# Attention layer, 64 units of a head pair: pair weights loaded one unit sooner, and outputs scaled by VectorE straight from PSUM

## The reference, cut to what matters

```python
h = einsum('od,bdl->bol', Wq[i], z[:, :, s:e]) + einsum('od,bdl->bol', Wi[i], u[:, :, s:e])   # i: columns 0-255, 256-511
q, k, v = split(h)                        # 16 heads x 64 x 512 columns each
prob = softmax(einsum('bndi,bndj->bnij', q + r_w_bias, k) / 8)
attn = einsum('bnij,bndj->bndi', prob, v)
x = Wo @ attn + bo + z                    # then a normalisation over the 256 rows
```

## Time and profile before

| | |
|---|---|
| median of three runs | 3446.04 us |
| the profiled execution's own time | 3442.56 us |
| its span, first to last instruction | 3440.5 us |
| mean granted TensorE clock | 0.949 |
| TensorE busy | 3115.6 us (91%) |
| VectorE busy | 2362.2 us (69%) |
| ScalarE busy | 1742.2 us (51%) |
| GpSimd busy | 701.2 us (20%) |
| first layer | up to about 1312 us |

### The profile page before, as it was taken

How to read it: one execution, slowest core, us unless ns; L and a number is a source line. 1 busy time by engine, 2 the same in 40 slices (tenths; PEclk the granted TensorE clock), 3 DMA queues, 4 the chain that set the end, 5 groups by cost and what they waited for, 6 DMA issues and landing times. The chain is left out here.

```text
span 3440.5 us, 55581 instructions
## 1 busy us (share of the span) xinstructions
PE 3115.6 (91%) x20384; PEld 2400.2 (70%) x20384; DVE 2362.2 (69%) x3589; ACT 1742.2 (51%) x4185; POOL 701.2 (20%) x1207
## 2 busy tenths in 40 slices
PE   7998999999998996799999997589999999699998
PEld 6777777777777774566666664378887787488885
DVE  6776666666675662999999999257777888543212
ACT  4454444544454543355566553247777777432222
POOL 2444444544444441000000000011101111000000
PEclk9999999999999998899999998789999999899999
DMA  7668766666675655445555444210011110310004
GB/s 245 209 218 268 225 184 183 207 212 197 197 234 162 207 143 187 121 96 123 116 117 120 104 109 104 59 64 14 26 56 56 44 44 29 108 50 12 25 13 167
DMA packets 179676, 434.78 MB, mean 126 GB/s; under 512 B 52912, under 2 KB 61104, under 8 KB 154960
## 3 DMA queue, kind: packets, MB, share of 16 engines
q1 hardware_dynamic: 120256, 262.17, 26.9%
q10 hardware_dynamic: 28304, 106.09, 8.6%
q0 software_dynamic: 30848, 62.97, 7.3%
HBM read 233.95 MB, written 62.91 MB: 86 GB/s over the span
## 5 line engine op out<-in xcount | busy, mean ns | idle before, releaser
L281 POOL DMA_DIRECT2D l_probT<-l_prob x896 | 441.2, 500 | 258.6 <-DVE l_prob L778 238.8
L756 DVE TENSOR_REDUCE l_nmax<-l_bank 128x1 f32<-128x512 f32 x512 | 317.0, 681 | 198.2 <-PE l_bank L453 198.2
L576 ACT ACTIVATE l_prob<-l_bank,l_nmax 128x512 f32<-128x512 f32 x512 | 344.5, 688 | 135.1 <-DVE l_nmax L756 120.5
L419 PE MATMUL l_bank<-l_x_hi,l_w_hi 128*128 128x256 f32 x1024 | 307.6, 300 | 75.4 <-DMA l_w_lo<-kept_w_lo 54.5
L778 DVE STREAM_TRANSPOSE l_prob<-l_prob 128x1024 f32<-128x1024 f32 x256 | 314.4, 1228 | 16.3 <-DVE l_acc L799 9.7
L419 PE MATMUL l_bank<-l_x_hi,l_w_lo 128*128 128x256 f32 x1024 | 299.8, 293 | 0.0
L419 PE MATMUL l_bank<-l_x_lo,l_w_hi 128*128 128x256 f32 x1024 | 299.0, 292 | 0.0
L1817 DVE TENSOR_TENSOR_SCAN l_kv<-l_wx,l_kv 128x2056 f32<-128x2056 f32 x64 | 283.8, 4435 | 3.1 <-DVE l_sxc L1938 1.5
L419 PEld LDWEIGHTS l_bank<-l_x_hi,l_w_hi 128*128 128x128 f32 x1024 | 207.0, 202 | 99.5 <-DMA l_w_lo<-kept_w_lo 59.2
L2391 ACT ACTIVATE l2a_sc<-l2a_sc,l2a_nmax 128x256 f32<-128x256 f32 x512 | 254.7, 508 | 41.1 <-DVE l2a_nmax L2507 41.1
L478 PE MATMUL l_bank<-l_probT,l_v 128*64 128x256 f32 x2048 | 248.6, 397 | 25.9 <-issue 12.5
(11 more groups left out here) (348 smaller groups left out, 7989.3 us busy)
## 6 DMA issues: line engine op xcount, KB each, us to landing
l_probT<-l_prob SPq DMA_DIRECT2D x1152, 64.0 KB, 2.7
l_vb<-vd SPq DMA_DIRECT2D x64, 1024.0 KB
l_probT<-l_prob POOLq DMA_DIRECT2D x896, 64.0 KB, 2.4
l_w_hi<-kept_w_hi ACTq DMA_DIRECT2D x24, 1024.0 KB, 7.2
l_w_lo<-kept_w_lo ACTq DMA_DIRECT2D x24, 1024.0 KB, 7.7
l_wv_hi<-kept_wv_hi ACTq DMA_DIRECT2D x12, 1024.0 KB, 5.4
l_wv_lo<-kept_wv_lo ACTq DMA_DIRECT2D x12, 1024.0 KB, 5.6
kept_w_hi<-l_w_hi SPq DMA_DIRECT2D x8, 1024.0 KB, 9.8
```

The source lines that it names most:

```text
L281: eng.dma_start(probT[i % RING][r * SQ:(r + 1) * SQ, g, :, :, :, :], prob[i % RING][g * SQ:(g + 1) * SQ, r * IT:(r + 1) * IT, :, :, :]).th ...
L419: mm = pe.matmul(s.ap[:, c * ROWS:(c + 1) * ROWS], a[:, kt, c, g, :], b[:, kt, c * ROWS:(c + 1) * ROWS], start=m == 0, stop=m == 3 * KT - 1)
L576: act.activation(prob[i % RING][:, :, it % 2, h, :].rearrange("p (q t) s -> p t q s", q=Q), s.ap[:, :].rearrange("p (t q s) -> p t q s", t ...
L756: dve.tensor_reduce(nmax[:, n % 2, it, h:h + 1], s.ap[:, :], AX.X, ALU.max, negate=True).then_inc(max_ready, 1)
```

## The change

Three edits, all in the first layer.

1. `load_w` takes t = n // 2 + 2 and part l instead of t = (n - 1) // 2 + 2 and part 1 - l. The high part of t is issued in step 2t - 4 and the low part in 2t - 3. It waits for the key product of unit 2t - 3 only. The value weights have a function of their own, `load_wv`, in the steps in which they were issued before (2t - 3 and 2t - 2), now behind the w load of that step.
2. `weighed` and `outputs` of ScalarE and `scale_outputs` of GpSimd are gone. VectorE's `outputs(n)` multiplies o{n} in PSUM by rT twice, once into oT_hi (rounded) and once into oT, and subtracts. The bank o{n} is thus released by VectorE's second product.
3. VectorE's `outputs(n - 2)` moves in step n from behind `queries(n + 1)` to behind `maxima(n, (0, 1))`, ahead of the first two transposes. ScalarE's `sums(n)` waits for the release of o{n - 1} where it waited for GpSimd's product.

```diff
@@ GpSimd
-                def scale_outputs(n):
-                    drained(pool, S[f"o{n}"])
-                    drained(pool, S[f"r{n}"])
-                    pool.tensor_tensor(oT[:, :], oT[:, :], rT[:, :], ALU.mult).then_inc(scaled, 1)
-
                 for n in range(HALF + 2):
-                    if n > 1:
-                        scale_outputs(n - 2)
@@ ScalarE
                 def sums(n):
                     s = S[f"r{n}"]
                     full(act, s)
-                    act.wait_ge(scaled, n)
+                    if n:
+                        drained(act, S[f"o{n - 1}"])
                     act.activation(rT[:, :], s.ap[:, :], ACT.Copy).then_inc(s.drained, 1)
-
-                def weighed(n):
...
-                    act.activation(oT[:, :], s.ap[:, :], ACT.Copy).then_inc(s.drained, 1)
-
-                def outputs(n):
...
-                    act.activation(oT_hi[:, :], oT[:, :], ACT.Copy).then_inc(oT_hi_ready, 1)
@@
                 def load_w(t, part):
                     p, i = t % HP, t % 2
-                    projected(act, LANES * (t - 2) + 1)
-                    if i == 0:
-                        act.wait_ge(wv_stored, 32 * QUADS)
-                        act.dma_start((wv_hi, wv_lo)[part][:, :, :, :, :].bitcast(F32), wv_scratch[part][p // 2]).then_inc(wv_in, 16)
+                    full(act, S[f"k{LANES * (t - 2) + 1}"])
                     act.wait_ge(w_stored[i], 32 * QUADS)
                     act.dma_start((w_hi, w_lo)[part][i][:, :, :, :, :].bitcast(F32), w_scratch[part][p]).then_inc(w_in[i], 16)
+
+                def load_wv(g, part):
+                    projected(act, LANES * 2 * (g - 1) + 1)
+                    act.wait_ge(wv_stored, 32 * QUADS)
+                    act.dma_start((wv_hi, wv_lo)[part][:, :, :, :, :].bitcast(F32), wv_scratch[part][g % QUADS]).then_inc(wv_in, 16)
@@
-                    t = (n - 1) // LANES + 2
+                    t = n // LANES + 2
                     if HP <= t < TURNS * HP:
-                        load_w(t, 1 - l)
+                        load_w(t, l)
+                    t -= 1 - l
+                    if HP <= t < TURNS * HP and t % 2 == 0:
+                        load_wv(t // 2, 1 - l)
@@ VectorE
                 def outputs(n):
+                    s = S[f"o{n}"]
+                    full(dve, s)
+                    drained(dve, S[f"r{n}"])
+                    if n:
+                        full(dve, S[f"w{n - 1}_{RT - 1}"])
+                    dve.tensor_tensor(oT_hi[:, :], s.ap[:, :], rT[:, :], ALU.mult).then_inc(oT_hi_ready, 1)
+                    dve.tensor_tensor(oT[:, :], s.ap[:, :], rT[:, :], ALU.mult).then_inc(s.drained, 1)
+                    drained(dve, s)
                     dve.wait_ge(oT_hi_ready, n + 1)
                     dve.tensor_tensor(oT_lo[:, :], oT[:, :], oT_hi[:, :].bitcast(F32), ALU.subtract).then_inc(oT_ready, 1)
@@
                     maxima(n, (0, 1))
+                    if n > 1:
+                        outputs(n - 2)
                     turns(n, 0)
                     turns(n, 1)
                     if n + 1 < HALF:
                         queries(n + 1)
-                    if n > 1:
-                        outputs(n - 2)
```

More of the change, by code:

```diff
@@ L238, in l0_attention @@
         max_ready, rinv_ready, rows_ready = ph.sem("max_ready"), ph.sem("rinv_ready"), ph.sem("rows_ready")
-        scaled, oT_ready = ph.sem("scaled"), ph.sem("oT_ready")
+        oT_ready = ph.sem("oT_ready")
         acc_in = [ph.sem(f"acc_in{l}") for l in range(LANES)]
@@ L603, in sums @@
                     full(act, s)
-                    act.wait_ge(scaled, n)
+                    if n:
+                        drained(act, S[f"o{n - 1}"])
                     act.activation(rT[:, :], s.ap[:, :], ACT.Copy).then_inc(s.drained, 1)
-                def weighed(n):
[L608 to L611, removed]
-                    act.activation(oT[:, :], s.ap[:, :], ACT.Copy).then_inc(s.drained, 1)
-                def outputs(n):
-                    act.wait_ge(scaled, n + 1)
-                    if n:
-                        full(act, S[f"w{n - 1}_{RT - 1}"])
-                    act.activation(oT_hi[:, :], oT[:, :], ACT.Copy).then_inc(oT_hi_ready, 1)
                 def split_x(bp, l):
@@ L734, in _ @@
                         centred()
-                    if n:
-                        weighed(n - 1)
                     if n + 1 < HALF:
@@ L742, in _ @@
                         normed()
-                outputs(HALF - 2)
                 sums(HALF - 1)
-                weighed(HALF - 1)
-                outputs(HALF - 1)
                 act.wait_ge(xn_ready, RT)
```

## The result

| | before | after |
|---|---|---|
| median, us (4 runs each) | 3446.64 (3442.6 to 3448.65) | 3394.32 (3388.02 to 3410.31) |
| the profiled execution's own time | 3442.56 | 3398.0 |
| its span | 3440.5 | 3395.9 |
| mean granted TensorE clock | 0.949 | 0.953 |
| TensorE, VectorE busy | 3115.6, 2362.2 us | 3117.0, 2431.1 us |

The before column holds one run more than the three of the median 3446.04 (its time is 3447.24). The changed kernel is faster by 52 us: the ratio of the times is 0.9857, with a 95% interval of [0.982, 0.9893]. The forecast was 3406, so the gain is 12 us larger than predicted.

What follows compares the result with a forecast made beforehand. TensorE, busy 91%, was taken as the bound, losing time mostly to waits for the low weight part. Terms: -75 + 9.6 + 5 + 8.5 + 8 + 3.5 = -40.4 us, giving 3406 us, range 3384 to 3429.

Steps and rivals of the forecast that it cites:

- Loads one unit sooner: Ten long steps and step 51: TensorE's waits for the low weight part disappear, -75 us.
- ScalarE's copies and GpSimd's product go: First layer: TensorE's waits don't come from them, so removing them gains 0 us.
- The new wait of the key product: Steps 4g and 4g + 1 from step 16: k's bank waits for VectorE's second product, 0.4 us in 24 steps, +9.6.
- The input split: Steps 31 and alike: VectorE's late split of the next x is exposed by 1.6 us, three times, +5 (3 to 8).
- The moves behind the change of turn: Steps 19 and 35: 18 moves queue behind SyncE's wait for the stored accumulator, 4.2 us waited again, +8.5 (5 to 13).
- Turn 0: VectorE's added work delays weight splits, and a w load joins the stores of step 12: +8 us (2 to 14).
- Small ones: Steps 50 to 54 wait for ends 0.6 us later, +2; moves landing late in some long steps, +1.5; together +3.5.
- VectorE sets the pace: Rival, short steps: VectorE's load above 14.7 us per unit bounds the kernel, 3462 us; chance 5%.
- the early load collides: Rival, ten long steps: moves of the probabilities land later, weighing waits some 2.5 us each, 3431 us; chance 12%.
- the givebacks are hidden: Rival: the added costs stay at their lower bounds, 12 us, so the gain is 63, 3383 us; chance 16%.
- the load doesn't arrive sooner: Rival: a semaphore on ScalarE's queue holds the weight load, 3461 us; chance 2%.

Runs made afterwards that it cites:

- the loads alone: The kernel before with only the earlier weight loads (edit 1), ScalarE's copies and GpSimd's product kept: 3392.06 us, ratio 0.9855.
- the products alone: The changed kernel with the old `load_w`, so VectorE's products and the new place of `outputs` without the earlier loads: 3459.12 us, ratio 1.0047.
- the second trace: Trace of the changed kernel run again, unaltered, as the measure for later versions: 3400.14 us, ratio 0.9866.
- the last experiment: Changed kernel with next x's load moved, its split sooner, w's first high-part reload in step 13, outputs ahead of maxima from turn 1: 3380.72 us, ratio 0.9806.
- 1.15 us more: The changed kernel with two further VectorE subtractions per unit into tiles that nobody reads: 3420.76 us, ratio 0.9929.
- the outputs first: The changed kernel with VectorE's `outputs(n - 2)` ahead of the first maxima in all turns: 3399.67 us, ratio 0.9867.

## Why the prediction was right, point by point

The time fell as forecast, for the reason forecast: the waits for the weights went, and part of what they had covered came back. By terms, from the traces:

- *Loads one unit sooner, -75.* Steps 23, 39, 43, 59 at 20.67 us and the loads alone at 3392 us show it. No low part arrives late. Of what the Trainium skill says of the clock (TensorE: Matmul & The Clock Gate, "Loop structure matters more than you think"), the direction is borne out: without the waits the clock stays at 1.00 in these four steps.
- *ScalarE's copies and GpSimd's product go, 0.* In turns 1 to 3 right. In turn 0 wrong: steps 4 and 8 wait for moves, and they are shorter with the products in both pairs of kernels (28.5 and 28.0 before against 24.7 and 25.4 with the products alone). The way is not the one that the prediction named, that GpSimd's moves start sooner. In the traces GpSimd's moves for the first half have landed 1.0 us (before) and 1.2 us (after) into step 4, and SyncE's nine, which the prediction took as hastened by nothing, land last, at 16.2 and 12.8 (15.8 in the second trace after); SyncE issues the last move of the second half at 14.8 us before and at 7.4 and 7.3 after. Why SyncE gets through sooner no run shows.
- *The new wait of the key product, +9.6.* Measured 0.27 for most of the 24 and 1.1 us in step 32: 7.0 in 22 steps, 7.3 in all. I had taken 0.4 for each. Why step 32 waits longer stays open; it took 20.9 to 22.5 us in the traces with `outputs` in its new place. The cause is shown from both sides by the position of `outputs`.
- *The input split, +5.* Measured 5.7. The size was right, the split of it not: 1.7 of each 1.9 is there without the products.
- *The moves behind the change of turn, +8.5 (5 to 13).* This is the term that was mis-sized: 7.6 + 7.5 = 15.1, above its own upper bound. The path was right. In step 35 the last of the 18 moves goes out 12.3 us into the step, as the prediction has it (12.2), but takes 6.2 us to land, not 4.9; in step 19 the store lands 2.3 us into the step, not 0.4, and the 18 moves with it. So TensorE waits 5.4 and 6.0 us there in place of 4.2, and the other 2.1 and 1.6 us are the clock, which falls to 0.88. That traffic holds the store up is shown in the experiments; I had taken its landing from one row.
- *Turn 0, +8 (2 to 14).* Measured +2.8. Steps 3, 7, 11 grew by 1.5 to 1.7 each, step 12 by 3.4 and step 0 by 2.7; steps 4 and 8 gave back 7.9, which I had not seen, and step 14 1.4. Step 0's share is chance: its wait of 3.7 us is the same, only the clock is at 0.84, and it took 19.6 in the second trace and 18.4 in the last experiment.
- *Small ones, +3.5.* Steps 50 to 54 +1.6, of which step 50 is 1.7 (same wait, lower clock, and 17.75 us again in the second trace, so chance), and step 27 +1.3. The waits of 5.03 and 3.97 us in steps 54 and 52 did not grow, so the mechanism that I gave them, ends of steps that come 0.6 later, was wrong.

Together they give -41.3 at the start of step 63, where the sum said -40.4. That it fits within 0.9 us is in part luck: the moves came 6.6 us above their term and turn 0 5.2 below it, the key's wait 2.3 below. In the second trace step 63 starts at 1239.0, 1.4 us later. The 12 us between forecast and median are thus not in the steps: 0.9 there, 3.3 behind step 63 (in this one trace), and 7.5 in the median, which I had put 3.8 above the profiled execution (3406 to 3402.2, much as it was before) and which is 3.7 below it.

The rivals: *VectorE sets the pace* is refuted for the change, since the short steps keep their 14.72 us (and all but one from step 17 on with 1.15 us more); *the early load collides* happened in step 12, and at most in one of the ten steps: 27 waits 1.5 us for a move, and takes 20.67 us with the loads alone; *the givebacks are hidden* is refuted, since they came to some 33 us and not to 12; *the load doesn't arrive sooner* is refuted.

What stays open: what happens between step 63 and the second layer's first accumulation. It takes 109.1 us in both traces of the changed kernel, 110.9 before, 114.7 with the loads alone, 115.9 with the outputs first. Step 63 of the kernel with the loads alone starts 14.8 us sooner than that of the changed kernel, and its median is only 2.3 us lower; so a first layer that is some microseconds shorter was not always a shorter execution. No run here takes that apart.

## What to carry to other kernels

A wait that ends last may be removed by issuing its DMA one iteration sooner, but price what it hid: here an input split (5.7 us) and the moves at a change of turn (15.1 us). Both paths could be read from the trace before, the full size of the second could not. When a buffer's release is moved to another engine, its new place in that engine's order decides: with the same three instructions TensorE waits 0, 0.27 or 3.6 us in each step in which it needs the buffer, depending only on what stands ahead of them. And when transfers share engines that are full, moving one may only move the wait, as it did from step 12 to step 14. A stretch in which the DMA share is low (0.38 in step 25) would be the place to try; no run here did.

## What the runs showed of the hardware that I had not expected

- A store of 0.5 MB that lands in 7.8 us took 19.5 when nine small moves were issued directly behind it, and 4.7 when a 1 MB load ahead of it was gone.
- The same wait can cost different amounts. In step 50, TensorE waits 2.51 us in both kernels. In the trace before, the step took 17.75 us at clock 1.00; in the first trace after, it took 19.44 at 0.91. It isn't the change that does it: in the changed kernel's second trace the step took 17.75 us at clock 1.00 again. The two windows:

```profile
1014.58:1032.33 17.75, 15.67 (x126) 12.53 (x124) 13.51 (x19) 8.52 (x22) 8.66 (x16) 1.00 0.96 317
```

```profile
979.58:999.02 19.44, 17.36 (x125) 13.30 (x123) 14.54 (x21) 7.41 (x20) 7.50 (x16) 0.91 0.94 311
```

- A VectorE product from PSUM took 0.68 us and the subtraction of two SBUF tiles 0.69: reading one operand from PSUM cost nothing extra here.
